# SyncE's queue reordered, the fourth block of the second norm moved into the next chunk, first diagonals shared between two engines: a state-space layer with an FFN on 8 cores

## What is computed

```python
x_dbl = einsum('bld,kd->blk', x, x_proj_w)         # 128 + 16 (B) + 16 (C)
delta = softplus(einsum('blr,dr->bld', x_dbl[..., :128], dt_proj_w) + dt_proj_b)
state = exp(delta * A) * state + delta * B * x     # over the tokens, 16 states a channel
y = sum_n(state * C) + x * D_param
x = layernorm(x + y)
out = einsum('bln,nk->blk', x, weight) * scale
v = max(norm(out), 1e-7); out = out * tanh(v) / (v + 1e-7)
out = out * min(0.99 / max(norm(out), 1e-7), 1)
x = layernorm(x + out)
```

## Time and profile before

| what | value |
|---|---|
| median of 3 runs | 1345.97 us (1341.26 to 1349.43) |
| profiled execution, its own time | 1349.57 us |
| its span, slowest core (core 2) | 1348.0 us |
| spans of the eight cores | 1333.7 to 1348.0 us |
| VectorE busy | 1189.6 us, 88% |
| GpSimd busy | 1034.5 us, 77% |
| ScalarE busy | 1000.8 us, 74% |
| TensorE busy | 964.9 us, 72% |

### The profile page before, as it was taken

How to read it: one execution, slowest core, us unless ns; L and a number is a source line. 1 busy time by engine, 2 the same in 40 slices (tenths; PEclk the granted TensorE clock), 3 DMA queues, 4 the chain that set the end, 5 groups by cost and what they waited for, 6 DMA issues and landing times.

```text
span 1348.0 us, 26244 instructions; the slowest of 8 cores (1333.7 to 1348.0 us)
## 1 busy us (share of the span) xinstructions
PE 964.9 (72%) x7952; PEld 573.4 (43%) x7952; DVE 1189.6 (88%) x610; ACT 1000.8 (74%) x1721; POOL 1034.5 (77%) x672
## 2 busy tenths in 40 slices
PE   3466566776688996776689986766699976658870
PEld 0344444444355553443355553444355544334330
DVE  2999899999998999999989999999999999994014
ACT  2566677777766889998667889998677989993144
POOL 2588678888897788999997788999997788994000
PEclk9588888988889998887889998887899998888995
DMA  7478567562569843233679743233468432324853
GB/s 105 94 129 133 97 111 111 106 100 55 114 123 158 148 103 60 68 92 67 115 129 169 146 91 55 69 96 87 90 138 161 120 77 40 95 68 113 186 123 124
DMA packets 267768, 143.80 MB, mean 107 GB/s; under 512 B 243376, under 2 KB 251760, under 8 KB 265328
## 3 DMA queue, kind: packets, MB, share of 16 engines
q1 hardware_dynamic: 258384, 124.17, 44.0%
q0 software_dynamic: 9248, 17.96, 9.6%
HBM read 84.34 MB, written 25.23 MB: 81 GB/s over the span
## 4 chain that ended last, share of the span: by engine, by line
DVE 26%; issue 22%; ACT 19%; POOL 12%; PE 11%; DMA 6%; SPq 3%; ACTq 0%; DVEq 0%; POOLq 0%
DVE h L1081 24%; ACT dae_x L837 9%; POOL g L428 7%; ACT dae_x L835 5%; PE pb L745 5%; DMA w_sl<-wbf 4%; PE pa L668 2%; POOL diagB L439 2%; POOL r_b L532 2%; POOL u_b L403 1%; SPq L332 1%; DMA x_b<-xT 1%; PE pb L631 1%; PE pb L650 1%; PE pb L633 1%
## 5 line engine op out<-in xcount | busy, mean ns | idle before, releaser
L428 POOL TENSOR_TENSOR g<-h,C_rep 128x1024 bf16<-128x1024 bf16 x384 | 813.3, 2130 | 159.0 <-DVE h L1081 140.3
L1081 DVE TENSOR_TENSOR_SCAN h<-dae_x,state,pa 128x1024 bf16<-128x1024 f32 x384 | 863.6, 2323 | 27.8 <-ACT dae_x L837 13.8
L668 PE MATMUL pa<-diagB,uT 128*128 128x128 bf16 x4096 | 371.4, 238 | 261.4 <-DVE h L1081 248.9
L835 ACT ACTIVATE dae_x<-delta,c_A 128x512 f32<-128x512 bf16 x512 | 367.3, 717 | 214.3 <-DVE h L1081 213.4
L668 PEld LDWEIGHTS pa<-diagB,uT 128*128 128x128 bf16 x4096 | 286.5, 106 | 452.2 <-issue 434.4
L837 ACT ACTIVATE dae_x<-delta,c_A 128x511 f32<-128x511 bf16 x512 | 361.9, 707 | 0.0
L1081 DVE TENSOR_TENSOR_SCAN h<-dae_x,pa 128x1024 bf16<-128x1024 f32 x128 | 281.1, 2264 | 5.8 <-PE pa L668 5.1
L745 PE MATMUL pb<-r_b,w_sl 128*128 128x512 bf16 x1024 | 260.1, 385 | 20.4 <-DMA w_sl<-wbf 20.3
L631 PE MATMUL pb<-g,eye_b 128*128 128x512 bf16 x384 | 168.3, 438 | 32.9 <-POOL g L428 17.0
L633 PE MATMUL pb<-g,eye_b 128*128 128x512 bf16 x384 | 167.4, 436 | 0.0
L745 PEld LDWEIGHTS pb<-r_b,w_sl 128*128 128x128 bf16 x1024 | 97.8, 99 | 134.7 <-issue 34.4
(11 more groups left out here) (127 smaller groups left out, 675.8 us busy)
## 6 DMA issues: line engine op xcount, KB each, us to landing
w_sl<-wbf SPq DMA_DIRECT2D x80, 512.0 KB, 4.3
out<-r_b SPq DMA_DIRECT2D x13, 1024.0 KB, 4.3
x_b<-xT POOLq DMA_DIRECT2D x16, 512.0 KB, 8.7
wbf<-wsw POOLq DMA_DIRECT2D x16, 512.0 KB, 6.4
C_rep<-bcscr SPq DMA_DIRECT2D x24, 256.0 KB, 6.1
hT<-h SPq DMA_TRANSPOSE x128, 3.3
out<-diagB SPq DMA_DIRECT2D x2, 1024.0 KB, 5.2
uT<-u_b SPq DMA_TRANSPOSE x64, 2.5
```

The lines of the kernel that those rows point to most:

```text
L428: e.tensor_tensor(s.g[:, g % NG, :, :], s.h[:, p, :, :], s.C_rep[:, GP.index(p), :, :], ALU.mult).then_inc(S["cmul"], 1)
L668: mm = e.matmul(s.ps_b[:, k % 2, n, tb * 128:(tb + 1) * 128], s.uT[:, j % 3, tb, :], s.diagB[:, p, tb, n, :], start=True, stop=True, skip_ ...
L835: e.activation(s.dae_x[:, k % 3, 0, :], s.delta[:, j % 3, :], AF.Exp, scale=s.c_A[:, n:n + 1])
L1081: e.tensor_tensor_scan(s.h[:, p, :, :].rearrange("p n t -> p (n t)"), s.dae_x[:, k % 3, :, :].rearrange("p n t -> p (n t)"), s.ps_b[:, k % ...
```

## The change

**SyncE's queue.** FFN weight loads (`load_w`, formerly `sync_w`) stand first in their step, ahead of the transposes; the first two of a chunk move from steps 0 and 1 to 2 and 3. The transpose of `u_b` moves from p = 5 for tile j+2 to p = 3 for tile j+1, so it asks for a product that GpSimd was given seven steps before, not one. In chunks 1 to 3 the 16 transposes of `r_b` stand at steps 14, 17, ... 59 (before 16, 18, ... 46); in the tail they stay.

**Token blocks.** For the tokens of chunks 0 to 2 the four blocks start at steps 93, 104, 115 and 135, that is step 7 of the chunk after the next (before 90, 98, 106, 114). Sums and small values move 3 to 12 steps later with them. The tail's own numbers stay.

**Head.** VectorE makes the first four `diagB` (`NH = 4`), GpSimd the other four and both `diagC`, after its two `u_b`.

```diff
-S_SRR = (52, 54, 56, 60)
-S_R2 = 90
-R2_GAP = 8
+RT_GAP = (3, 2)
+S_SRR = ((62, 65, 68, 71), (52, 54, 56, 60))
+S_R2 = ((93, 104, 115, 135), (90, 91, 92, 93))
+NH = 4
...
+def r2_at(k, after):
+
+    for c in range(NCH):
+        for tb in range(NTB):
+            if (c + 1) * STEPS + r2_step(c, tb) + after == k:
+                return c, tb
+    return None
...
         for k in range(END):
             c, st = divmod(k, STEPS)
             j, p = divmod(k, NP)
+            if c > 0 and st in (2, 3):
+                s.load_w(e, c * NKT + st - 2)
+            for kt in range(2, NKT):
+                if c > 0 and st == kt_done(kt - 2):
+                    s.load_w(e, c * NKT + kt)
             if k < NK and p - 1 in TP:
                 s.sync_ht(e, j, TP.index(p - 1))
-            if p == 5 and j + 2 < NJ:
-                s.sync_ut(e, j + 2)
+            if p == 3 and 2 <= j + 1 < NJ:
+                s.sync_ut(e, j + 1)
...
+        i, off = divmod(st - S_RT[c == LAST], RT_GAP[c == LAST])
+        if off == 0 and 0 <= i < NDT:
+            s.sync_rt(e, c, i)
...
+        for p in range(NH, NP):
+            s.diag_b(e, 0, p, S["diag"])
+        for w in range(2):
+            s.diag_c(e, 0, w)
...
+            hit = r2_at(k, 1)
+            if hit and hit[0] < LAST:
+                s.gpsimd_r2(e, *hit)
...
+        if r2_at(k, 3):
+            s.scalar_r2sq(e, *r2_at(k, 3))
...
-        for p in range(NP):
-            s.diag_b(e, 0, p)
-        for w in range(2):
-            s.diag_c(e, 0, w)
+        for p in range(NH):
+            s.diag_b(e, 0, p, S["diag_h"])
```

More of the change, by code:

```diff
@@ L42 @@
     "nmr", "o_ev", "o_ev_v",
-    "a_neg", "diag_d", "diag", "diag_c", "scan", "row", "row_t", "r2", "r2_t",
+    "a_neg", "diag_d", "diag_h", "diag", "diag_c", "scan", "row", "row_t", "r2", "r2_t",
     "cmul", "u",
@@ L270, in sync_tokens, with sync_out @@
                 ).then_inc(S["et1" if n % 2 else "et0"], 16)
[L271 to L280, removed]
+    def sync_out(s, e, c, tb):
+        S = s.sem
+        row = c * TL + tb * 128
+        if c == LAST and tb >= 2:
+            e.wait_ge(S["o_ev_v"], tb - 1)
+        else:
+            e.wait_ge(S["o_ev"], c * NTB + tb + 1)
+        e.dma_start(out=s.out_d[row:row + 128, :], in_=s.r2(c, tb)
+                    ).then_inc(S["out_st"], 16)
     def sync_ht(s, e, j, w):
@@ L354, in gpsimd_program @@
         s.gpsimd_u(e, 1)
-        for k in range(NK + 1):
+        for p in range(NH, NP):
+            s.diag_b(e, 0, p, S["diag"])
+        for w in range(2):
+            s.diag_c(e, 0, w)
+        for k in range(NK + S_FFN):
             c, st = divmod(k, STEPS)
             j, p = divmod(k, NP)
-            if k > 0 and (k - 1) % NP in GP:
+            if 0 < k <= NK and (k - 1) % NP in GP:
                 s.gpsimd_cmul(e, k - 1)
@@ L662, in tensor_b @@
         if j % NDT == 0:
-            e.wait_ge(S["diag"], c * NP + p + 1)
+            if c == 0 and p < NH:
+                e.wait_ge(S["diag_h"], p + 1)
+            else:
+                e.wait_ge(S["diag"], c * NP + p + 1 - NH)
         if k >= 2:
@@ L918, in scalar_tokens @@
                     accum_out=t("srr")[:, col]).then_inc(S["srr"], 1)
-            if st == S_SEE[tb] and not (c == LAST and tb >= 2):
+            if st == S_SEE[c == LAST][tb] and not (c == LAST and tb >= 2):
                 if tb == 0:
@@ L974, in scalar_tokens, with scalar_r2, after_row @@
-        for tb in range(NTB):
-            if st == r2_step(c, tb) + 5 and not (c == LAST and tb >= 2):
-                col = slice(tb, tb + 1)
-                e.wait_ge(S["nmr"], n_a2(c, tb))
-                act(s.r2(c, tb), s.r2(c, tb), AF.Identity,
-                    scale=t("rq")[:, col], bias=t("nmr")[:, col]
-                    ).then_inc(S["o_ev"], 1)
+    def scalar_r2(s, e, k):
+        S = s.sem
+        act = e.activation
+        t = s.t
+        def after_row(c, name, tb=None):
+            e.wait_ge(S["row" if c < LAST else "row_t"], n_row(c, name, tb))
+        hit = r2_at(k, 0)
+        if hit and hit[0] < LAST:
+            c, tb = hit
+            after_row(c, "ff")
+            act(s.eT[:, tb, :], s.eT[:, tb, :], AF.Copy,
+                scale=t("ff")[:, tb:tb + 1],
+                accum_out=t("r2sum")[:, tb:tb + 1]).then_inc(S["fe"], 1)
+        if r2_at(k, 3):
+            s.scalar_r2sq(e, *r2_at(k, 3))
+        if r2_at(k, 4):
+            c, tb = r2_at(k, 4)
+            col = slice(tb, tb + 1)
+            n = n_a2(c, tb)
+            after_row(c, "bq", tb)
+            e.wait_ge(S["sq"], n)
+            act(t("lnq")[:, col], t("r2sq")[:, col], AF.Ln, scale=RD,
+                bias=t("bq")[:, col]).then_inc(S["lnq"], 1)
+            e.wait_ge(S["lnq"], n)
+            act(t("rq")[:, col], t("lnq")[:, col], AF.Exp, scale=-0.5
+                ).then_inc(S["rq"], 1)
+            e.wait_ge(S["rq"], n)
+            act(t("nmr")[:, col], t("nm")[:, col], AF.Copy,
+                scale=t("rq")[:, col]).then_inc(S["nmr"], 1)
+        hit = r2_at(k, 5)
+        if hit and not (hit[0] == LAST and hit[1] >= 2):
+            c, tb = hit
+            col = slice(tb, tb + 1)
+            e.wait_ge(S["nmr"], n_a2(c, tb))
+            act(s.r2(c, tb), s.r2(c, tb), AF.Identity,
+                scale=t("rq")[:, col], bias=t("nmr")[:, col]
+                ).then_inc(S["o_ev"], 1)
@@ L1053, in vector_last @@
         s.token_values(e, LAST, st, S["row_t"])
-        for tb in range(NTB):
-            if st == r2_step(LAST, tb) + 2:
-                s.vector_r2(e, tb)
+        hit = r2_at(NK + st, 2)
+        if hit and hit[0] == LAST:
+            s.vector_r2(e, hit[1])
         for tb in (2, 3):
```

77 lines of the change are left out of this document (26 added, 51 removed).

## The result

The changed kernel takes 1357.7 us (median of 6 runs), the kernel before 1348.0 beside it (6 runs). The ratio is 1.0091, with a 95% interval of 1.005 to 1.0133: slower by 0.9%. (Disturbed runs are left out of the ratios here, not out of the medians; one of 1368.11 us, with a lower clock on four cores, still counts, and without it the ratio of the means is 1.0075.) The profiled execution took 1357.05 us.

A forecast was written before the change was run, and what follows sets the result against it. VectorE bounds the chunks, the FFN on TensorE the tail. Losses 33.7 less gains 25.6 give net +8.1 us: 1357.7 for the profiled execution, 1354 for the median; range 1342 to 1364.

The forecast's parts named there:

- Step 13: Chunks 2 and 3: scan waits 9.1 us for exponentials queued behind the fourth block's squares, which wait for GpSimd's late add.
- rival 1: Fourth block at step 7: ScalarE never waits for it, since GpSimd's backlog is below 3.9 us; 1330 us, chance 0.12.
- Until scan 15: Chunks 2 and 3: the late mean makes scan 15 12.4 us late, 11.9 net per chunk, 23.8 in all.
- Tail: Fourth block stands ahead of the mean: FFN 8.2 us later, 1.7 for the clock; two weight loads gain 2.4.
- Head: Before the first scan: four diagonals on VectorE are enough to begin, gain 5.9 us, bounds 4.8 to 6.7.
- The queue: SyncE: loads first and an older `u_b` end TensorE's weight waits, 8.5 us in chunks 1 and 2, 1.5 in chunk 0.
- Chunk 1: All TensorE waits of this chunk but the one at step 18 go with the queue order, 5.4 us.
- Step 18: Chunk 1: `C_rep` on time stops GpSimd making TensorE late, 1.0 us gained of a 1.5 us wait.
- Chunk ends: Four blocks at 8 steps overload ScalarE; wider spacing cuts 10.5 us of waits to 4.2, gain 6.3, bounds 2 and 10.5.
- Rival 3: SyncE's queue: the gain doesn't come and the 8.5 us of weight waits stay; 1362.5 us, chance 0.15.

The follow-up runs named there:

- e3: Changed kernel with the fourth block's squares, small values, output and write-out seven steps later, its scaling and add left in place: 1334.6 us, ratio 0.9899.
- e4: Changed kernel with GpSimd's add of the fourth block covering only 128 of 2048 channels: 1347.0 us, one run.
- e9: Changed kernel with the token steps of before and the weight loads in their old place: median 1336.7 us, ratio 0.993.
- e11: Kernel before with only the `u_b` transposes moved, to step 3 of a group and one tile ahead: 1340.3 us, ratio 0.995.
- e1: Changed kernel with the token steps of before; new queue order and shared head stay: 1332.9 us, ratio 0.9886.
- e5: Changed kernel with the fourth block's squares and what follows seven steps later, and chunk 2's four blocks at steps 93, 101, 109, 117: 1329.8 us, ratio 0.9872.
- e8: Changed kernel with the token steps of before and the `u_b` transposes in their old place: 1341.5 us, ratio 0.9948.
- e12: Kernel before with only the weight loads in their new place, ahead of the other transposes: 1344.2 us, ratio 0.9982.
- e2: Changed kernel with weight loads and `u_b` transposes back in their old places in the queue: 1368.4 us, ratio 1.0178.
- e6: Changed kernel with all four token blocks of every chunk at steps 93, 101, 109 and 117: 1331.3 us, ratio 0.9881.
- e10: Changed kernel with the four token blocks ten steps apart, at 93, 103, 113 and 123: 1340.9 us, ratio 0.995.

## Why the prediction was right, term by term

The forecast was 1354 for the median and 1357.7 for the profiled execution; they are 1357.7 and 1357.05. The sum came out as it should, several of its terms did not. Part of the closeness is luck. The sum was built on core 2 of before, the slowest, whose span is 7.2 us over that of the median core; the slowest of the changed kernel is 0.9 over. So the slowest cores grew by 7.5 us, forecast 8.1, and the median core by 13.8.

- **Step 13.** The first wait, 9.1 us forecast, is 9.23 in chunk 2 and 9.24 in chunk 3, with the chain as described; e3 and e4 show that it hangs on ScalarE's place behind the add and on the add's length. GpSimd's backlog behind scan 7 was 13.0 us and 18.0 behind scan 8. The sum had 13.1 for the first (669.0 less 655.9, with `C_rep` on time); the 15.4 of rival 1 is the same with `C_rep` late, and the lower bound of 8.5, given for a backlog of 13, has no ground, since at 13.1 the sum itself gives 9.1.
- **Until scan 15.** 9.23 + 0.29 + 2.60 = 12.1 us, forecast 12.4, less what it covers. Chunks 2 and 3 as a whole: +7.9 and +8.7 over the median core, forecast +6.7 and +9.8 with their gains, the 6.3 us of the chunk ends shared evenly over three chunks.
- **Tail.** The mean was evicted at 1244.22, 15.6 us after the last scan, where it had been 8.1: 7.4 later, forecast 8.2. ScalarE at the start of the tail, where the earlier trace rows have only the first and the last of these:

```profile
1232.14 0.60 ACT L902 ACTIVATE r_b<-pb 128x512 bf16<-128x512 f32 x1 [5.73 <-PE pb L660]
1232.64 1.99 ACT L992 ACTIVATE eT<-eT,tok 128x2048 bf16<-128x2048 bf16 x1
...
1239.06 1.91 ACT L1026 ACTIVATE eT<-r_b 128x2048 bf16<-128x2048 f32 x1 [4.34 <-POOL r_b L556]
...
1242.23 2.09 ACT L1016 ACTIVATE r_b<-r_b,tok 128x2048 f32<-128x2048 f32 x1
1244.22 0.57 ACT L919 ACTIVATE mean_b<-pb 128x512 bf16<-128x512 f32 x1
```

The clock was granted 0.82 as before, so the 1.7 us for it had no ground; nor had the 2.4 gained by the queue, since without that block the tail's median core is 115.9 to 116.3 us with the loads in their old place (before, e9, e11) and 114.8 to 116.6 with them in the new one (e1, e5 to e8, e12). But the block costs more than its delay of the mean: +10.7 in all on the median core. 6.2 of that is still there in e3 (122.8), where the squares, output and write-out come after the mean. That they and their DMAs crowd the FFN's transposes and weights is only argued; no run separates them. On the two profiled cores the tail came to +7.8, where 7.5 was forecast: that agreement is owed to a slow tail on the core shown of before (119.1 against a median of 116.3).
- **Head.** 5.1 us, forecast 5.9, bounds 4.8 to 6.7. The fourth VectorE diagonal took 2.92 us beside GpSimd's first of 2.88; I had allowed 1.1 to 3.0 for it and taken about the middle (which is 5.75, not 5.9). GpSimd's six ended at 49.1, not near 46, and chunk 0 is as long either way. The Trainium skill (SBUF — State Buffer, on the shared port pair) has the two lock each other out for whole instructions, which gave 4.8; the trace is nearer to it than to my value.
- **The queue.** The step that failed, though its size held: "The change puts the load first and asks for an older `u_b`, so the 4 us of delay go." Both halves were given the credit, and beside the other the load's place has little of it: without it e9 is 1.3 us above e1 in the median core's span (3.8 in the runs' medians, with intervals that overlap), and alone it gains 0.2% (e12). Most is the `u_b` transpose, which no longer stops the queue: alone it gains 0.5% (e11), 8.2 us of the median core's span, of which 4.0 in chunk 0. The 3.1 us for chunk 2 were core 2's own, too: the median core of before waits 1.3 at that step. Chunk 0 gained 4.4 us over the median core (2.4 on the one shown), forecast 1.5: I had counted one transpose less ahead of the load, and it was the slow landing behind a transpose of `u_b`.
- **Chunk 1.** 9.5 us on the slowest core, forecast 8.5, but 5.1 on the median core. About half is the chunk's end (last item). For the other half there is more than one cause that suffices: without the new token steps the `u_b` transposes give 2.8 (e11) and the loads 1.9 (e12), and with them neither is needed (e2). Cores that wait over 1 us for TensorE after step 20 of the chunk: seven in before, four each in e8 and e12, two in e2, one in e11, none in e1, e9 and the changed kernel. The 4.37 us stall of the earlier trace rows stands on core 2 alone; the other seven cores of before wait 0.5 to 4.5 us for TensorE in chunk 1, where core 2 waits 6.9.
- **Step 18.** The 1.0 us rested on a late `C_rep` that makes TensorE late. In the changed kernel no product of GpSimd waits 0.5 us for `C_rep` on any core, yet five of the eight cores wait 1.53 us for TensorE at step 18 of chunk 1, where before only core 2 did (1.50). So the cause was named wrongly; what ends that wait was not taken apart. That it fell to 0.51 on core 2 is luck.
- **Chunk ends.** Waits of 0.84 and 0.94 (chunk 1), 0.83 and 0.95 (chunk 2) and 0.73 us (chunk 3) are left of the 10.5: 4.3, forecast 4.2; the second of each pair is for TensorE. With four blocks in the chunk (e6) they are 4.4, 4.5 and 1.8. Number and spacing both count. The first three blocks of chunk 1 wait 3.3 us at 8 steps apart (e6), 1.6 at 10 (e10) and 1.8 at 11; the fourth of e6 waits 1.15. VectorE in e6, from step 117 of chunk 1 to step 6 of chunk 2:

```profile
595.45 18.01 DVE L1117 TENSOR_TENSOR_SCAN h<-dae_x,state,pa 128x1024 bf16<-128x1024 f32 x8 [1.31 <-ACT dae_x L865]
614.61 20.25 DVE L1117 TENSOR_TENSOR_SCAN h<-dae_x,state,pa 128x1024 bf16<-128x1024 f32 x9 [1.15 <-ACT dae_x L865]
636.77 2.35 DVE L1117 TENSOR_TENSOR_SCAN h<-dae_x,state,pa 128x1024 bf16<-128x1024 f32 x1 [1.91 <-POOL g L451]
```

The last wait, for GpSimd's product, is 0.40 in the changed kernel. So a fourth block kept in the chunk costs about 2.7 us (1.15 and 1.5), and several times as much elsewhere.

Rival 1 (ScalarE never waits) failed on the backlog, 13.0 us against the 3.9 at which it decides. Rival 3 (the queue's gain doesn't come) failed too.

## What to carry to other kernels

Work that one in-order engine does for another should stand where the maker is ahead: the same block costs the bound engine about 2.7 us in two waits when it starts at step 117, but in one wait of 8.7 at 123 and of 9.2 at 135, with more behind it. There the add's engine is 9.4 and 13.0 us behind (2.3 at 117), and the consumer has its own urgent work behind the wait. In a DMA queue look for the request that is made before its data exist; moving it later helps everything behind it, and moving the victim to the front of its own step does little here (0.2%). And read the other cores before a stall of the slowest one is counted as a gain.
